# Token-id expert layer of a two-layer decoder: operands as exact sums of two 12-bit parts, products as three one-pass products of the parts, not native 32-bit ones

## The chip, the cores and the metric

The kernel runs on one core of one Trainium2 chip. The metric is device time in microseconds (us) for one execution. Times are medians of runs; the profile is of one execution.

## The reference, cut to what matters

The program is a decoder of two layers with six sublayers, each followed by a residual sum and a layer norm: a gated linear recurrence (stage A in the kernel), the token-id expert layer (B), a mixture of experts (C), window attention (D), a quantised product with the context (E), and latent attention with experts (F, G). The change is in stage B only:

```
expert_ids = jnp.minimum(tid // tokens_per_expert, E - 1)      # E = 4, one expert for each token
for e in range(E):
    g = jax.nn.silu(jnp.einsum('bsd,fd->bsf', hidden_states, Wg[e]))
    u = jnp.einsum('bsd,fd->bsf', hidden_states, Wu[e])
    y = jnp.einsum('bsf,df->bsd', g * u, Wd[e])
    out = jnp.where((expert_ids == e)[..., None], y, out)
...
x = _layernorm(x + _L0_xattn_ref(x, itok_BxS_13_99985, ctx_2048, ctx_2048, ctx_2048), axis=-1)
```

There are 2048 tokens of 512 features. All three weights of expert e are the same 512 x 512 matrix (ctx_2048[e]), so one product with it gives both g and u, and a second product with it gives y. The hidden value is silu(v) * v, which the kernel takes as (1 + tanh(v/2)) * v * v, with the factor 1/2 put into the residual sum.

## The kernel before, in words

Stage A has sorted the tokens by expert into 19 tiles of 128 rows (TILES_B = 19), each of one expert, has loaded the four transposed matrices into w (128 partitions x 4 experts x 4 chunks x 512, float32), and has left the tables row, who and tile_expert. An all-engine barrier ends it. Stage B is tokenid_expert_layer. No planner sets its order: each engine has its instructions in the order written, and semaphores tie the engines together.

- POOL (GpSimd) gathers tile n's rows of x1 into xg, a ring of four (AHEAD = 4, line 707). gather(n + 4) is issued after the sum of tile n is made (sum_ready) and, since POOL works in order, behind the small power for the inverse deviation of tile n (line 719). It scatters the finished rows into x2 (line 712).
- PE (TensorE) works in rounds. Round n holds, in this order: turn_x(n + 1), four transposes of 128x128 (line 765); turn_h(n - 1), four transposes (line 774); first_product(n), four calls of a 128x128 by 128x512 product (line 786); second_product(n - 1), four calls (line 796). The expert's number is read into a register, which addresses w.
- DVE (VectorE) in its loop for n: keep_xT(n + 1), the copy of the transposed rows out of PSUM (line 823); normalise(n - 2) (line 844); hidden(n) (line 827); moments(n - 1), which is the residual sum (line 832, it frees xg for the next gather), the statistics (835, 836) and the addition of epsilon (837).
- ACT (ScalarE): keep_hT(n - 1), the copy of the transposed hidden rows (line 749), then tanh and square of the first product of n (lines 741, 742).

PSUM has two buffers for each of the four uses (banks 0 to 7). Stage C begins after stage B's barrier.

Of the kernel before, what the change touches and what calls it, by code (L numbers as in the profile page):

```python
# [15 lines left out]
P = 128  # L16
# [3 lines left out]
KD = D // P  # L20
# [4 lines left out]
F32 = mybir.dt.float32  # L25
BF16 = mybir.dt.bfloat16
# [637 lines left out]
def tokenid_expert_layer(nc, d, x1, x2, route, ident):  # L664
# [5 lines left out]
    with stage_of(nc) as ctx:  # L670
# [6 lines left out]
        def sems(name):  # L677
# [3 lines left out]
        w, who, row, tile_expert = route  # L681
        power = sb("power", [P, 1])
        xg = [sb(f"xg{j}", [P, D]) for j in range(AHEAD)]
        res, y = ([sb(f"{n}{j}", [P, D]) for j in range(AHEAD)] for n in ("res", "y"))
        xgT, hT = ([sb(f"{n}{j}", [P, KD, P]) for j in (0, 1)] for n in ("xgT", "hT"))
# [5 lines left out]
        (x_turned, xT_ready, product1, th_ready, sq_ready, h_ready, h_turned, hT_ready, product2, sum_ready, var_ready, rstd_ready,  # L691
         y_ready) = (sem(n) for n in (
            "x_turned", "xT_ready", "product1", "th_ready", "sq_ready", "h_ready", "h_turned", "hT_ready", "product2",
            "sum_ready", "var_ready", "rstd_ready", "y_ready"))
        dve_step, power_ready = sem("dve_step"), sem("power_ready")
# [38 lines left out]
        @block.scalar  # L734
        def _(act):
            def squares(n):
                act.wait_ge(product1, n + 1)
                if n >= 2:

                    act.wait_ge(h_turned, n - 1)  # L740
                nc.scalar.activation(th[n % 2][:], ps[:, 2 + n % 2, :], ACT.Tanh, scale=0.5).then_inc(th_ready, 1)
                nc.scalar.activation(sq[n % 2][:], ps[:, 2 + n % 2, :], ACT.Square).then_inc(sq_ready, 1)

            def keep_hT(n):
                act.wait_ge(h_turned, n + 1)
                if n >= 2:

                    act.wait_ge(product2, n - 1)
                nc.scalar.copy(hT[n % 2][:], ps[:, 4 + n % 2, :].rearrange("p (k m) -> p k m", k=KD)).then_inc(hT_ready, 1)

            for n in range(TILES_B + 1):
                if n >= 1:
                    keep_hT(n - 1)
                if n < TILES_B:
                    squares(n)

        @block.tensor
        def _(pe):
            def turn_x(n):
                pe.wait_ge(gathered[n % AHEAD], 16 * (n // AHEAD + 1))  # L760
                if n >= 2:

                    pe.wait_ge(xT_ready, n - 1)
# [4 lines left out]
            def turn_h(n):  # L768
                pe.wait_ge(h_ready, n + 1)
                if n >= 2:  # L770

                    pe.wait_ge(hT_ready, n - 1)
# [6 lines left out]

            def first_product(n, e):  # L780
                pe.wait_ge(xT_ready, n + 1)
                if n >= 2:

                    pe.wait_ge(sq_ready, n - 1)
                for k in range(KD):
                    last = nc.tensor.matmul(ps[:, 2 + n % 2, :], xgT[n % 2][:, k, :], w[:, bass.ds(e, 1), k, :],
                                            start=(k == 0), stop=(k == KD - 1))
                last.then_inc(product1, 1)

            def second_product(n, e):  # L790
                pe.wait_ge(hT_ready, n + 1)
# [3 lines left out]
                for k in range(KD):  # L795
                    last = nc.tensor.matmul(ps[:, 6 + n % 2, :], hT[n % 2][:, k, :], w[:, bass.ds(e, 1), k, :],
                                            start=(k == 0), stop=(k == KD - 1))
                last.then_inc(product2, 1)

            e_now = expert(0)  # L800
            turn_x(0)
            for n in range(TILES_B + 1):
# [12 lines left out]
        def _(dve):  # L815
            steps = Steps(dve, dve_step)

            def keep_xT(n):
                dve.wait_ge(x_turned, n + 1)
# [3 lines left out]
                nc.vector.tensor_copy(xgT[n % 2][:], ps[:, n % 2, :].rearrange("p (k m) -> p k m", k=KD)).then_inc(xT_ready, 1)  # L823
# [23 lines left out]
            keep_xT(0)  # L847
            for n in range(TILES_B):
                if n + 1 < TILES_B:
                    keep_xT(n + 1)  # L850
# [5 lines left out]
            normalise(TILES_B - 2)  # L856
            moments(TILES_B - 1)
# [2711 lines left out]
```

## Time and profile before

| | |
|---|---|
| median of 3 runs | 2498.16 us (2497.85 to 2498.19) |
| profiled execution, first to last instruction (the only time that is kept of it) | 2498.3 us |
| busy share: PE, PE weight load, DVE, ACT, POOL | 90%, 41%, 55%, 26%, 28% |
| stage B, first gather to last scatter's issue | 391.8 to 552.3 us |
| lines 786 and 796, the two products: records of each | 152 (8 for each tile) |

How to read it: "PE" rows are matmuls, "PEld" rows the loads of the stationary operand, which overlap them. A matmul's listed duration includes the time through the array, so matmuls in a row overlap each other; what one costs in a row of them is the distance between starts. A float32 product of this form appears as two records. TensorE's clock has two levels, 1.2 and 2.4 GHz; the profile gives the granted share, 0.50 or 1.00, or a mean. In a timeline row the columns are start, duration, engine, line, operation, output <- inputs, count, and in brackets the idle time before it with what ended it. The program's span is the sum of its stages; between stages stands a barrier.

### The profile page before, as it was taken

How to read it: one execution, taken by the hardware profiler on the slowest of the kernel's cores; microseconds unless marked ns; L12 is line 12 of the kernel's file. 1: busy time of each engine (PE TensorE's matmuls, PEld its weight loads, DVE VectorE, ACT ScalarE, POOL GpSimd, SP SyncE). 2: the span in 40 equal slices, each digit the busy share in tenths (PEclk: the TensorE clock that was granted, in tenths of full speed). 3: DMA queues.
4: the chain of work that ended last, by engine and by line, in shares of the span. 5: the costliest groups of instructions: out<-in, count | busy, mean ns of one | idle time of the engine just before them, and what ended most of it. 6: DMA issues, size and time to landing. Idle time of an engine off the chain costs nothing. (4 is left out here: it accounts for less than half of the span.)

```text
span 2498.3 us, 29517 instructions
## 1 busy us (share of the span) xinstructions
PE 2247.5 (90%) x10083; PEld 1030.3 (41%) x10086; DVE 1381.1 (55%) x3181; ACT 657.9 (26%) x1163; POOL 695.2 (28%) x1018
## 2 busy tenths in 40 slices
PE   9999997979999999898999997478888888799993
PEld 4444443435444443344444443233333333344441
DVE  6999883436412223555766774955656564422224
ACT  2222321212012121233434333433322322002223
POOL 2210002324523321133433333011113131125553
PEclk9999998999999999998999998689999999999997
DMA  8333102126047776163443330310000000064444
GB/s 293 117 101 112 40 4 72 64 76 243 10 133 247 236 234 202 40 165 83 90 85 78 84 71 2 109 71 1 2 18 2 18 27 18 17 199 83 87 88 149
DMA packets 101697, 235.40 MB, mean 94 GB/s; under 512 B 18919, under 2 KB 42647, under 8 KB 94399
## 3 DMA queue, kind: packets, MB, share of 16 engines
q1 hardware_dynamic: 79006, 191.83, 24.4%
q0 software_dynamic: 22560, 41.87, 7.7%
q8 instruction: 77, 1.26, 0.2%
q14 instruction: 54, 0.43, 0.1%
HBM read 174.69 MB, written 63.53 MB: 95 GB/s over the span
## 5 line engine op out<-in xcount | busy, mean ns | idle before, releaser
L1876 DVE CUSTOM_DVE_ANT_0 D_ps<-D_ps,D_mask 128x256 f32<-128x256 f32 (+1 forms) x512 | 186.9, 420 | 70.7 <-PE D_ps L1773 69.7
L1625 POOL TENSOR_SCALAR_AFFINE_SELECT D_probs<-D_probs 128x256 f32<-128x256 f32 x256 | 106.1, 420 | 286.7 <-ACT D_probs L1683 286.4
L1683 ACT ACTIVATE D_probs<-D_ps 128x512 f32<-128x512 f32 (+1 forms) x256 | 125.3, 543 | 165.0 <-PE D_ps L1795 164.8
L2876 DVE TENSOR_REDUCE F_neg_max<-F_ps 128x4 f32<-128x2048 f32 (+1 forms) x64 | 93.9, 1488 | 107.7 <-PE F_ps L2774 101.6
L3318 PE MATMUL G_ps<-G_gate_up,G_xgT 128*128 x304 | 138.5, 599 | 0.3 <-DVE G_xgT L3409 0.3
L2626 ACT ACTIVATE F_probs<-F_ps 128x1536 f32<-128x1536 f32 (+1 forms) x48 | 76.4, 1591 | 187.2 <-PE F_ps L2790 187.2
L1186 PE MATMUL C_ps<-C_down_shared,C_hs 128*128 128x512 f32 x256 | 114.0, 593 | 3.4 <-DVE C_hs L1353 2.3
L1174 PE MATMUL C_ps<-C_xT,C_gate_shared 128*128 128x512 f32 x256 | 115.4, 593 | 0.6 <-ACT C_xT L1049 0.6
L1174 PE MATMUL C_ps<-C_xT,C_up_shared 128*128 128x512 f32 x256 | 115.1, 592 | 0.0
L1773 PE MATMUL D_ps<-D_k_stack,D_q_stack 96*128 96x256 bf16 (+1 forms) x512 | 93.4, 268 | 8.8 <-DVE D_maxima L1876 7.2
L1023 POOL DMA_INDIRECT expert_sums<-C_y,C_of_slot x32 | 50.2, 1570 | 173.4 <-ACT C_y L1090 108.9
L2507 POOL TENSOR_SCALAR_AFFINE_SELECT F_probs<-F_probs 128x512 f32<-128x512 f32 x64 | 41.0, 652 | 179.7 <-ACT F_probs L2626 179.7
L3417 DVE SCALAR_TENSOR_TENSOR G_tile_gu<-G_tile_th,G_ps 128x256 f32<-128x256 f32 x38 | 16.0, 421 | 129.9 <-ACT G_tile_th L3230 129.9
L374 PE MATMUL A_ps<-A_u,A_wa 128*128 128x512 f32 x200 | 86.5, 592 | 0.0
L374 PE MATMUL A_ps<-A_u,A_wi 128*128 128x512 f32 x200 | 86.5, 592 | 0.0
L1795 PE MATMUL D_ps<-D_q_stack,D_k_stack 99*128 99x256 bf16 (+1 forms) x512 | 75.3, 272 | 12.3 <-DMA D_q_stack<-D_m_lo 12.3
L1811 PE MATMUL D_ps<-D_probs,D_v 128*32 128x256 f32 (+1 forms) x1024 | 78.2, 378 | 6.5 <-POOL D_probs L1627 4.8
L1005 POOL DMA_INDIRECT slots<-C_entry,C_address x64 | 64.3, 1004 | 55.2 <-DVE C_address L1338 36.6
L1773 PEld LDWEIGHTS D_ps<-D_k_stack,D_q_stack 96*128 96x128 bf16 x512 | 44.6, 101 | 84.3 <-issue 51.2
L3318 PEld LDWEIGHTS G_ps<-G_gate_up,G_xgT 128*128 128x128 f32 x304 | 55.4, 192 | 56.1 <-issue 56.1
L1627 POOL TENSOR_SCALAR_AFFINE_SELECT D_probs<-D_probs 128x256 f32<-128x256 f32 x192 | 77.9, 406 | 0.0
L1795 PEld LDWEIGHTS D_ps<-D_q_stack,D_k_stack 99*128 99x128 bf16 x512 | 47.3, 101 | 67.9 <-issue 39.5
(496 smaller groups left out, 4531.1 us busy)
## 6 DMA issues: line engine op xcount, KB each, us to landing
C_ring<-moe_experts_dram SPq DMA_DIRECT2D x32, 1536.0 KB, 6.9
qk_parts<-D_parts SPq DMA_DIRECT2D x32, 384.0 KB, 2.5
B_w<-ctx_dram SPq DMA_DIRECT2D x8, 1024.0 KB, 6.0
expert_sums<-A_cq SPq DMA_DIRECT2D x1, 8192.0 KB, 29.4
C_ring<-expert_sums SPq DMA_DIRECT2D x5, 1536.0 KB, 10.4
D_q_stack<-qk_parts SPq DMA_DIRECT2D x16, 384.0 KB, 4.8
D_k_stack<-qk_parts SPq DMA_DIRECT2D x16, 384.0 KB, 7.7
B_w<-ctxT_dram SPq DMA_DIRECT2D x1, 4096.0 KB, 15.9
```

The lines of the kernel that those rows point to most:

```text
L374: last = nc.tensor.matmul(ps[:, tile % 8, :], w[:, k, m * P:(m + 1) * P], moving[:, k, :], start=(k == 0), stop=(k == chunks - 1))
L1174: last = nc.tensor.matmul(ps[:, bank + part, :], w_shared[part][:, k, f:f + P], xT[:, k, g * S:(g + 1) * S], start=(k == 0), stop=(k == KD ...
L1186: last = nc.tensor.matmul(ps[:, 2 + c % 2, :], hs[:, m, i * P:(i + 1) * P], down_shared[:, s * KF + m, :], start=(m == 0), stop=(m == KF - 1))
L1625: last = nc.gpsimd.affine_select(now[:, :, 0:P], now[:, :, 0:P], [[0, 2], [1, P]], ALU.is_ge, 0.0, base=0, channel_multiplier=-1)
L1627: last = nc.gpsimd.affine_select(now[:, :, P:2 * P], now[:, :, P:2 * P], [[0, 2], [-1, P]], ALU.is_ge, 0.0, base=0, channel_multiplier=1)
L1683: nc.scalar.activation(probs[at % 2][:, 2 * pair:2 * pair + 2, 0:w], ps[:, 4 + unit % 3, :].rearrange("p (h q) -> p h q", h=2)[:, :, 0:w], ...
L1773: last = nc.tensor.matmul(ps[:, 2 + u % 2, h * 256 + first:(h + 1) * 256], q_stack[0:STACK, head, t * P:(t + 1) * P], k_stack[0:STACK, hea ...
L1795: last = nc.tensor.matmul(bank[:, h * 256:h * 256 + w], k_stack[:, head, kb * P:(kb + 1) * P], q_stack[:, head, kb * P:kb * P + w], start= ...
L1811: last = nc.tensor.matmul(ps[h * (P // 4):(h + 1) * (P // 4), 7, kb * P:kb * P + w], v[b % 2][:, kb, c * HC + 4 * g + h, :], probs[at % 2] ...
L1876: last = nc.vector.tensor_tensor_reduce(now, now, mask[:, first:256], 1.0, -3e38, ALU.add, ALU.max, maxima[n % 2][:, head, t:t + 1])
L2876: last = nc.vector.tensor_reduce(neg_max[n % 2][:, :, t], ps[:, 0:GROUP, at:at + w], AX_X, ALU.max, negate=True)
L3318: last = nc.tensor.matmul(ps[:, 2 + a, :], xgT[a][:, k, :], gate_up[:, bass.ds(e, 1), k, :], start=(k == 0), stop=(k == KD - 1))
```

## The change

A product is then hi*hi + hi*lo + lo*hi, all in the float32r type, accumulated in one PSUM bank: 12 matmul calls in place of 4. The transposes stay float32.

- The weights are split once at the stage's head: four copies of 128x2048 on ACT, four subtractions on DVE. PE waits for all of them (w_lo_ready) after turn_x(0).
- For each tile ACT makes x_hi from PSUM (high_x) and h_hi in place of hT (high_h). DVE makes x_lo in place of the copy xgT (low_x), and h_lo (low_h), each after the high part.
- The last third of each product waits for the low part. In DVE's last steps low_h(18) stands behind normalise(17).

```
--- before.py
+++ after.py
@@ -23,6 +23,7 @@
 EPS = 1e-5
 
 F32 = mybir.dt.float32
+F32R = mybir.dt.float32r
 BF16 = mybir.dt.bfloat16
 I32 = mybir.dt.int32
 U32 = mybir.dt.uint32
@@ -679,20 +680,22 @@
 
         E, AHEAD = EXPERTS_B, 4
         w, who, row, tile_expert = route
+
+        w_hi, w_lo = (sb(n, [P, E, KD, D], F32R) for n in ("w_hi", "w_lo"))
         power = sb("power", [P, 1])
         xg = [sb(f"xg{j}", [P, D]) for j in range(AHEAD)]
         res, y = ([sb(f"{n}{j}", [P, D]) for j in range(AHEAD)] for n in ("res", "y"))
-        xgT, hT = ([sb(f"{n}{j}", [P, KD, P]) for j in (0, 1)] for n in ("xgT", "hT"))
+        x_hi, x_lo, h_hi, h_lo = ([sb(f"{n}{j}", [P, KD, P], F32R) for j in (0, 1)] for n in ("x_hi", "x_lo", "h_hi", "h_lo"))
         th, sq = ([sb(f"{n}{j}", [P, D]) for j in (0, 1)] for n in ("th", "sq"))
         stats, mv, rstd = sb("stats", [P, 6]), sb("mv", [P, TILES_B, 2]), sb("rstd", [P, TILES_B])
         ps = ctx.enter_context(nc.psum_tensor("B_ps", [P, 8, 512], F32))
 
         gathered, stored = sems("gathered"), sems("stored")
-        (x_turned, xT_ready, product1, th_ready, sq_ready, h_ready, h_turned, hT_ready, product2, sum_ready, var_ready, rstd_ready,
-         y_ready) = (sem(n) for n in (
-            "x_turned", "xT_ready", "product1", "th_ready", "sq_ready", "h_ready", "h_turned", "hT_ready", "product2",
-            "sum_ready", "var_ready", "rstd_ready", "y_ready"))
-        dve_step, power_ready = sem("dve_step"), sem("power_ready")
+        (x_turned, x_hi_ready, x_lo_ready, product1, th_ready, sq_ready, h_ready, h_turned, h_hi_ready, h_lo_ready, product2,
+         sum_ready, var_ready, rstd_ready, y_ready) = (sem(n) for n in (
+            "x_turned", "x_hi_ready", "x_lo_ready", "product1", "th_ready", "sq_ready", "h_ready", "h_turned", "h_hi_ready",
+            "h_lo_ready", "product2", "sum_ready", "var_ready", "rstd_ready", "y_ready"))
+        dve_step, power_ready, w_hi_ready, w_lo_ready = (sem(n) for n in ("dve_step", "power_ready", "w_hi_ready", "w_lo_ready"))
         block = ctx.enter_context(nc.Block(no_gpsimd_drain=True))
 
         @block.gpsimd
@@ -741,16 +744,28 @@
                 nc.scalar.activation(th[n % 2][:], ps[:, 2 + n % 2, :], ACT.Tanh, scale=0.5).then_inc(th_ready, 1)
                 nc.scalar.activation(sq[n % 2][:], ps[:, 2 + n % 2, :], ACT.Square).then_inc(sq_ready, 1)
 
-            def keep_hT(n):
+            def high_x(n):
+                act.wait_ge(x_turned, n + 1)
+                if n >= 2:
+
+                    act.wait_ge(product1, n - 1)
+                nc.scalar.copy(x_hi[n % 2][:], ps[:, n % 2, :].rearrange("p (k m) -> p k m", k=KD)).then_inc(x_hi_ready, 1)
+
+            def high_h(n):
                 act.wait_ge(h_turned, n + 1)
                 if n >= 2:
 
                     act.wait_ge(product2, n - 1)
-                nc.scalar.copy(hT[n % 2][:], ps[:, 4 + n % 2, :].rearrange("p (k m) -> p k m", k=KD)).then_inc(hT_ready, 1)
-
+                nc.scalar.copy(h_hi[n % 2][:], ps[:, 4 + n % 2, :].rearrange("p (k m) -> p k m", k=KD)).then_inc(h_hi_ready, 1)
+
+            for e in range(E):
+                nc.scalar.copy(w_hi[:, e].rearrange("p k n -> p (k n)"), w[:, e].rearrange("p k n -> p (k n)")).then_inc(w_hi_ready, 1)
+            high_x(0)
             for n in range(TILES_B + 1):
+                if n + 1 < TILES_B:
+                    high_x(n + 1)
                 if n >= 1:
-                    keep_hT(n - 1)
+                    high_h(n - 1)
                 if n < TILES_B:
                     squares(n)
 
@@ -760,7 +775,7 @@
                 pe.wait_ge(gathered[n % AHEAD], 16 * (n // AHEAD + 1))
                 if n >= 2:
 
-                    pe.wait_ge(xT_ready, n - 1)
+                    pe.wait_ge(x_lo_ready, n - 1)
                 for k in range(KD):
                     last = nc.tensor.transpose(ps[:, n % 2, k * P:(k + 1) * P], xg[n % AHEAD][:, k * P:(k + 1) * P], ident[:])
                 last.then_inc(x_turned, 1)
@@ -769,7 +784,7 @@
                 pe.wait_ge(h_ready, n + 1)
                 if n >= 2:
 
-                    pe.wait_ge(hT_ready, n - 1)
+                    pe.wait_ge(h_lo_ready, n - 1)
                 for k in range(KD):
                     last = nc.tensor.transpose(ps[:, 4 + n % 2, k * P:(k + 1) * P], sq[n % 2][:, k * P:(k + 1) * P], ident[:])
                 last.then_inc(h_turned, 1)
@@ -777,28 +792,34 @@
             def expert(n):
                 return pe.value_load(tile_expert[0:1, n:n + 1], min_val=0, max_val=E - 1)
 
+            def three_products(out, hi, lo, lo_ready, n, e):
+
+                for k in range(KD):
+                    nc.tensor.matmul(out, hi[:, k, :], w_hi[:, bass.ds(e, 1), k, :], start=(k == 0), stop=False)
+                for k in range(KD):
+                    nc.tensor.matmul(out, hi[:, k, :], w_lo[:, bass.ds(e, 1), k, :], start=False, stop=False)
+                pe.wait_ge(lo_ready, n + 1)
+                for k in range(KD):
+                    last = nc.tensor.matmul(out, lo[:, k, :], w_hi[:, bass.ds(e, 1), k, :], start=False, stop=(k == KD - 1))
+                return last
+
             def first_product(n, e):
-                pe.wait_ge(xT_ready, n + 1)
+                pe.wait_ge(x_hi_ready, n + 1)
                 if n >= 2:
 
                     pe.wait_ge(sq_ready, n - 1)
-                for k in range(KD):
-                    last = nc.tensor.matmul(ps[:, 2 + n % 2, :], xgT[n % 2][:, k, :], w[:, bass.ds(e, 1), k, :],
-                                            start=(k == 0), stop=(k == KD - 1))
-                last.then_inc(product1, 1)
+                three_products(ps[:, 2 + n % 2, :], x_hi[n % 2], x_lo[n % 2], x_lo_ready, n, e).then_inc(product1, 1)
 
             def second_product(n, e):
-                pe.wait_ge(hT_ready, n + 1)
+                pe.wait_ge(h_hi_ready, n + 1)
                 if n >= 2:
 
                     pe.wait_ge(sum_ready, n - 1)
-                for k in range(KD):
-                    last = nc.tensor.matmul(ps[:, 6 + n % 2, :], hT[n % 2][:, k, :], w[:, bass.ds(e, 1), k, :],
-                                            start=(k == 0), stop=(k == KD - 1))
-                last.then_inc(product2, 1)
+                three_products(ps[:, 6 + n % 2, :], h_hi[n % 2], h_lo[n % 2], h_lo_ready, n, e).then_inc(product2, 1)
 
             e_now = expert(0)
             turn_x(0)
+            pe.wait_ge(w_lo_ready, E)
             for n in range(TILES_B + 1):
                 if n + 1 < TILES_B:
                     e_next = expert(n + 1)
@@ -815,12 +836,21 @@
         def _(dve):
             steps = Steps(dve, dve_step)
 
-            def keep_xT(n):
-                dve.wait_ge(x_turned, n + 1)
+            def low_x(n):
+                dve.wait_ge(x_hi_ready, n + 1)
                 if n >= 2:
 
                     dve.wait_ge(product1, n - 1)
-                nc.vector.tensor_copy(xgT[n % 2][:], ps[:, n % 2, :].rearrange("p (k m) -> p k m", k=KD)).then_inc(xT_ready, 1)
+                nc.vector.tensor_tensor(x_lo[n % 2][:], ps[:, n % 2, :].rearrange("p (k m) -> p k m", k=KD), x_hi[n % 2][:].bitcast(F32),
+                                        ALU.subtract).then_inc(x_lo_ready, 1)
+
+            def low_h(n):
+                dve.wait_ge(h_hi_ready, n + 1)
+                if n >= 2:
+
+                    dve.wait_ge(product2, n - 1)
+                nc.vector.tensor_tensor(h_lo[n % 2][:], ps[:, 4 + n % 2, :].rearrange("p (k m) -> p k m", k=KD), h_hi[n % 2][:].bitcast(F32),
+                                        ALU.subtract).then_inc(h_lo_ready, 1)
 
             def hidden(n):
                 dve.wait_ge(sq_ready, n + 1)
@@ -844,16 +874,23 @@
                 nc.vector.tensor_scalar(y[n % AHEAD][:], res[n % AHEAD][:], mv[:, n, 0:1], rstd[:, n:n + 1],
                                         ALU.subtract, ALU.mult).then_inc(y_ready, 1)
 
-            keep_xT(0)
+            for e in range(E):
+                dve.wait_ge(w_hi_ready, e + 1)
+                nc.vector.tensor_tensor(w_lo[:, e].rearrange("p k n -> p (k n)"), w[:, e].rearrange("p k n -> p (k n)"),
+                                        w_hi[:, e].rearrange("p k n -> p (k n)").bitcast(F32), ALU.subtract).then_inc(w_lo_ready, 1)
+            low_x(0)
             for n in range(TILES_B):
                 if n + 1 < TILES_B:
-                    keep_xT(n + 1)
+                    low_x(n + 1)
+                if n >= 1:
+                    low_h(n - 1)
                 if n >= 2:
                     normalise(n - 2)
                 hidden(n)
                 if n >= 1:
                     moments(n - 1)
             normalise(TILES_B - 2)
+            low_h(TILES_B - 1)
             moments(TILES_B - 1)
             normalise(TILES_B - 1)
```

## Rows read from the trace of the kernel before

**Rows 1.** Stretches: length, busy PE, PEld, DVE, ACT, POOL, clock, DMA, GB/s.

```profile
474.58:482.32 7.74, 7.74 (x26) 3.87 (x25) 3.58 (x8) 1.67 (x3) 2.84 (x3) 1.00 0.20 68
396.87:402.34 5.47, 5.47 (x13) 2.81 (x14) 0.99 (x2) 0.00 (x0) 0.00 (x0) 0.71 0.21 79
```

**Rows 2.** Timeline of one round in the middle of stage B.

```profile
473.70 0.60 PE L765 MATMUL B_ps<-ident,B_xg 128*128 128x128 f32 x4
473.90 0.69 DVE L832 SCALAR_TENSOR_TENSOR B_res<-B_ps,B_xg 128x512 f32<-128x512 f32 x1 [1.63 <-PE B_ps L796]
474.14 0.60 PE L774 MATMUL B_ps<-ident,B_sq 128*128 128x128 f32 x4
474.58 3.60 PE L786 MATMUL B_ps<-B_w,B_xgT 128*128 x8
...
476.56 1.28 POOL L707 DMA_INDIRECT B_xg<-x,B_row  x1 [0.19 <-issue]
478.01 3.60 PE L796 MATMUL B_ps<-B_w,B_hT 128*128 x8
...
481.45 0.60 PE L765 MATMUL B_ps<-ident,B_xg 128*128 128x128 f32 x4
```

**Rows 3.** Line 707's gathers issued between 470 and 500 us.

```profile
DMA to landing us min/median/max: 3.6/3.7/3.8
```

**Rows 4.** Timeline of one-pass bf16 products at 256 columns (stage D).

```profile
1102.70 0.61 PE L1795 MATMUL D_ps<-D_q_stack,D_k_stack 99*128 99x256 bf16 x4 [1.00 <-DMA D_q_stack<-D_m_lo]
1103.14 0.28 PE L1773 MATMUL D_ps<-D_k_stack,D_q_stack 96*128 96x128 bf16 x2
```

**Rows 5.** Timeline of bf16 transposes at full clock (stage E).

```profile
1592.64 1.07 PE L2087 MATMUL E_turned<-E_ident,E_xq 128*128 128x128 bf16 x16 [2.70 <-DVE E_xq L2126]
```

**Rows 6.** Weight loads by tile in stage B: count, ns min/median/max, starts, forms.

```profile
L786 PEld LDWEIGHTS B_ps<-B_w,B_xgT x152: 190/190/333, 397.6 to 538.7; 128*128 128x128 f32 x152
L774 PEld LDWEIGHTS B_ps<-ident,B_sq x76: 139/140/143, 404.4 to 543.2; 128*128 128x128 f32 x76
```

**Rows 7.** Groups by line and shape: busy us, mean ns, idle before.

```profile
L538 DVE TENSOR_TENSOR B_w<-B_w 128x2048 f32<-128x2048 f32 x4 | 9.2, 2292 | 0.1
L2025 ACT ACTIVATE E_work<-rows,E_scale 128x2048 f32<-128x2048 f32 x4 | 8.0, 2016 | 21.2 <-DVE E_scale L2110 21.2
L1857 DVE TENSOR_TENSOR D_rest<-D_ps,D_parts 128x512 f32<-128x512 f32 x32 | 22.1, 690 | 29.2 <-ACT D_parts L1654 29.2
L749 ACT COPY B_hT<-B_ps 128x512 f32<-128x512 f32 x19 | 11.1, 585 | 58.6 <-PE B_ps L774 58.6
```

**Rows 8.** Timeline of the end of stage A and the head of B.

```profile
387.47 0.32 SPq L271 DMA_DIRECT2D x<-A_y  x1
391.79 1.19 POOL L707 DMA_INDIRECT B_xg<-x,B_row  x1 [4.93 <-issue]
...
396.87 1.11 PE L765 MATMUL B_ps<-ident,B_xg 128*128 128x128 f32 x4 [0.43 <-DMA B_xg<-x,B_row]
397.77 4.73 PE L786 MATMUL B_ps<-B_w,B_xgT 128*128 x8
...
402.34 0.60 PE L765 MATMUL B_ps<-ident,B_xg 128*128 128x128 f32 x4
...
404.40 0.66 PE L774 MATMUL B_ps<-ident,B_sq 128*128 128x128 f32 x4 [1.47 <-DVE B_sq L827]
...
411.76 0.60 PE L765 MATMUL B_ps<-ident,B_xg 128*128 128x128 f32 x4
```

**Rows 9.** Line 271's four stores at the end of stage A.

```profile
DMA to landing us min/median/max: 2.0/2.2/2.5
```

**Rows 10.** Timeline of the end of stage B.

```profile
544.23 3.70 PE L796 MATMUL B_ps<-B_w,B_hT 128*128 x8 [0.68 <-ACT B_hT L749]
...
545.66 0.55 DVE L844 TENSOR_SCALAR B_y<-B_res,B_mv,B_rstd 128x512 f32<-128x512 f32 x1 [0.69 <-POOL B_rstd L719]
...
547.96 0.69 DVE L832 SCALAR_TENSOR_TENSOR B_res<-B_ps,B_xg 128x512 f32<-128x512 f32 x1 [1.75 <-PE B_ps L796]
```

## The prediction

> **What bounds the kernel now.** I read the page of the profile first, then, for the stretch of stage B alone, the busy time by stretches, the groups by line, PE's waits and the timeline. The page calls PE busy for 90% of the span, but that is a mean over seven stages and the change touches one, so the first thing to see is a window of one round of stage B: 7.74 us long, PE busy for all 7.74 at a granted clock of 1.00 (2.4 GHz), DVE 3.58, ACT 1.67, POOL 2.84 [rows 1]. PE sets the period there. The timeline of a round shows how it is made up: four transposes take 0.44 us (473.70 to 474.14), the next four 0.44, the first product 3.43 (474.58 to 478.01), the second 3.44, and the next round starts at 481.45, a period of 7.75 [rows 2]. Each product is eight records, so a record costs 3.43 / 8 = 0.429 us for 512 columns, and a call two of them, 0.858.
>
> The second thing to see is what stands just behind PE. The residual sum frees the gather ring; it starts 0.20 us after the round's end (473.90), and the gather of the tile four further on is issued at 476.56, 2.86 us after the end [rows 2]. It lands 3.7 us later (3.6 to 3.8) [rows 3], at 6.56. Its transposes are due after one more round, at 7.75. So the gather has 1.2 us to spare today, and a shorter period uses that up.
>
> **The change, part by part.**
>
> *A pass.* In place of 8 records of 0.429 us a product has 12 of an unknown price p. The trace has no float32r product. Lower bound: four bf16 passes of 256 columns start 0.44 us apart from the next group (1102.70 to 1103.14), 0.11 each, hence 0.22 for 512 columns [rows 4]; and a native call divided by four is 0.858 / 4 = 0.2145. Upper bound: the only single-record 32-bit operations, the transposes, take 0.11 us for 128 columns [rows 2], where 16 bf16 transposes take 1.07 us with the last one's run-out, under 0.07 each [rows 5]. If 32-bit words of any kind move at that pace, p is 0.429. 
>
> The Trainium skill ("FP8 and Floating Point Precision", section TensorE Precision Notes) says that a true float32 product is four passes and that a reduced one reads four bytes and cuts them to 22 bits. By that rule three products of parts cost 3/4 of the native one; the native records, 0.858 for a call, agree with a count of four, and no run yet shows the reduced one.
>
> *Weight loads.* Each pass needs its own load. Loads take 190 ns in the native product and 139 ns in the transposes [rows 6], both under 214, and they overlap the matmul before. So they stay hidden; with no such cover the 139 would be added to every pass (below nothing is gained: the loads are hidden already).
>
> *Register work and waits on PE.* The second waits (for the low part) fall where the low part is ready: low_x(n) is made a round ahead, low_h(n - 1) as worked out next. In the trace no idle time stands between the transposes and the register-addressed product [rows 2], so I put the addresses at nothing; if 12 calls outran PE's sequencer, it would show as a larger p.
>
> *DVE and ACT in a round.* low_x replaces a copy at the same price, a subtraction of 128x512 out of PSUM, 690 ns; low_h adds one more, so DVE has 3.58 + 0.69 = 4.3 us. ACT has 1.67 + 0.59 = 2.3 us for one more copy of 585 ns [rows 1, 7]. Both lie under any period above. In order of time from the end of a round: moments until 2.0, low_x 2.7, low_h 3.5, normalise 4.1. PE wants h_lo at 0.88 + 2.57 + 1.72 = 5.2. It costs nothing, with 1.7 us of cover. The gather's path (sum, statistics, POOL) is ahead of all that was added, so it stays at 2.86 + 3.7.
>
> *The period.* PE alone: 0.88 + 24 x 0.2145 = 6.03 us. The gather lands 6.56 after the end of round n + 1, and turn_x(n + 4) opens round n + 3, which then takes 6.03 itself. Two rounds so cost 6.56 + 6.03, a period of 6.30. What was hidden becomes a wait of about 0.5 us before every second round's transposes (or half of it before each). Seventeen rounds, 2 to 18: 17 x (7.75 - 6.30) = 24.6 us gained; by PE alone 17 x 1.72 = 29.2.
>
> *The head.* PE waits for four low parts of the weights. DVE's subtraction of 128x2048 takes 2.29 us; the nearest row for the copy is an ACT activation from SBUF of the same size, 2.02 [rows 7]. DVE waits for the first copy only, so the split lasts 2.02 + 4 x 2.29 + 0.1 = 11.3 us. It starts with the stage, after the last store of stage A lands: 387.47 + 2.2 = 389.7 at the earliest, 391.79 (POOL's first gather) at the latest [rows 8, 9]; I take 390.3. PE enters round 0 at 401.6, not at 396.87: 4.8 us late (4.2 to 6.3). Round 0 took 5.47 us at a mean granted clock of 0.71 [rows 1] for 0.44 + 3.43 = 3.87 us of full-clock work, so 3.2 us of it ran at 1.2 GHz. PE is idle ahead of it again, so I keep these 3.2: 0.44 + 2.57 + 1.6 = 4.6 us, 0.9 less (if the clock doesn't rise at all, 6.0). Round 1 took 9.42 (402.34 to 411.76), with 2.06 from its start until the hidden rows are ready [rows 8]. Now 2.06 + 0.44 + 5.15 = 7.65, 1.8 less. The head together: +4.8 - 0.9 - 1.8 = +2.1.
>
> *The tail.* The last second product ran from 544.23, and its sum began at 547.96 [rows 10]. low_h(18) stands behind normalise(17), which ends at 545.66 + 0.55 = 546.21 on the old scale; h_lo comes at 546.9, four passes take 0.86, the sum starts at 548.0. With its first eight passes done long before, this costs 0.1 us.
>
> Sum: +2.1 - 24.6 + 0.1 = -22.4. The profiled execution's span is 2498.3 us, the median 2498.16, so 2475.8 by the median; I say 2476. The later stages start after a barrier and only move forward.
>
> **Rivals.**
> 1. *No wait for the gather* (it lands sooner, or the loop closes in another way): +2.1 - 29.2 + 0.1 = -27, 2471. For it: landings of 3.3 us would cut the period to 6.1. Against: none between 470 and 500 us was under 3.6 [rows 3].
> 2. *32-bit words move at half pace*, the one on the other side. p = 0.429, period 0.88 + 24 x 0.429 = 11.2: 17 x 3.4 = +58, head +4.8 + 1.7 + 3.4, tail +1.6, together +70, 2568. For it: the transposes [rows 2, 5]. The sum has p some 450 times (12 + 24 + 408 and the tail), so from -27 at 0.2145 it turns at 0.2145 + 27 / 450 = 0.274 us.
> 3. *Weight loads come into the open:* p = 0.2145 + 0.139 = 0.354, period 9.4, +36 together, 2534. Against: a load starts one matmul ahead today and is shorter than a pass [rows 6].
> 4. *The change doesn't do what it says:* a float32r call is run as a native one, 0.858. The period is 21.5, over 230 us slower, above 2730.
> 5. *Passes closer than their columns.* From the native rows, eight records of 0.429 leave no room for it [rows 2]; a pass of 0.131 would make PE's round 4.0, the gather's loop (6.56 + 4.0) / 2 = 5.3, and the whole 43 us faster, 2455. The Trainium skill ("TensorE: Matmul & The Clock Gate", section Back-to-back issue gap) gives such a 131 ns for streams of load and matmul at 512 columns; the trace disagrees, 0.2145 for a quarter of a call.
>
> **How the numbers follow.** Forecast 0.56, rival 1 0.22, rival 2 0.12, rival 3 (with smaller exposures or a slow sequencer) 0.06, rivals 4 and 5 0.01 each, and 0.02 for a p near 0.274, where gain and loss cancel. The forecast's own bounds: stage start and cold round +1.5 + 1.4 and -0.6, landings of 4.2 us in busier queues +4.3 (period 6.55). That gives 2475 to 2483; with rival 1 below it and some play on either side, 2468 to 2486 holds just under 8 in 10. A difference under 0.2% (5 us) is about what a measurement of this kernel can't tell from none. Faster 0.80, within it 0.02, slower 0.18.
>
> **What the changed profile would show.** In the middle of stage B: 12 records for each product, starts 0.21 apart, weight loads under 0.2 us; the granted clock at 1.00; a period of 6.2 to 6.4 with PE idle for the gather in line with the transposes of x, 0.2 to 0.6 us. At the head: four ACT copies of about 2.0, four DVE subtractions of 2.29, the first product at about 402.5, not 397.8. At the end: low_h(18) right behind normalise(17). The prediction is wrong if the records are 0.4 apart, if idle time stands ahead of each load, if PE waits for h_lo, or if the clock drops in mid-stage.

## The result, and the profile after

| | before | changed | ratio to before, 95% interval |
|---|---|---|---|
| first comparison | 2498.19 us (2497.85 to 2504.62) | 2487.24 us (2481.16 to 2489.70) | 0.9938 (0.9921 to 0.9955) |
| second | 2496.25 | 2485.66 | 0.9945 (0.9923 to 0.9967) |
| third | 2497.14 | 2479.85 | 0.9930 (0.9911 to 0.9948) |

The change makes the kernel 0.6% faster: 0.0062 x 2498.16 is 15.5 us, between 11.2 and 19.7. The forecast was 22.4 less, 2476 in a range of 2468 to 2486; by the ratio it is 2482.7, while the median of the changed kernel's own runs, 2487.24, lies 1.2 above that range. A second run of the unchanged kernel before came out at 1.0014 (1.0000 to 1.0028).

The profiled execution of the changed kernel has a span of 2479.4 us, against 2498.3. Its stage B lasts from 392.84 (the first gather) to 535.85 (the start of the last scatter), 143.0 us; the kernel before has 391.79 to 551.31, 159.5 us (the 552.3 in the table ahead of the prediction is the end of that last scatter's instruction). So 16.5 us came out of stage B, in that trace; in two more of the changed kernel B took 142.7 and 143.5, in a second one of before 160.4. The rest of the span's difference lies in stages that the change does not touch: stage C took 494.5 and 498.5 us in two traces of before, 491.7, 498.0 and 491.8 in three of the changed kernel; D goes from 513.6 to 517.5 in these five. B is read from traces to about 1 us, a whole execution is not.

The page of the changed kernel, busy time by engine: DVE rises from 55% to 57%, ACT from 26% to 27%.

```profile
PE 2218.7 (89%) x10235; PEld 1054.4 (43%) x10238; DVE 1401.2 (57%) x3204; ACT 675.1 (27%) x1186; POOL 695.5 (28%) x1018
```

One round in the middle of stage B, timeline of the changed kernel (line 780 is turn_x, 789 turn_h, 798/800/803 the three groups of passes, 852 low_h, 862 the sum, 710 the gather). It answers to [rows 2].

```profile
462.38 0.60 PE L780 MATMUL B_ps<-ident,B_xg 128*128 128x128 f32 x4
462.58 0.69 DVE L862 SCALAR_TENSOR_TENSOR B_res<-B_ps,B_xg 128x512 f32<-128x512 f32 x1 [0.99 <-PE B_ps L803]
...
463.17 1.18 PE L798 MATMUL B_ps<-B_w_hi,B_x_hi 128*128 x4
464.19 1.10 PE L800 MATMUL B_ps<-B_w_lo,B_x_hi 128*128 x4
464.94 0.68 DVE L852 TENSOR_TENSOR B_h_lo<-B_ps,B_h_hi 128x512 fp32r<-128x512 f32 x1
465.12 1.10 PE L803 MATMUL B_ps<-B_w_hi,B_x_lo 128*128 x4
465.25 1.01 POOL L710 DMA_INDIRECT B_xg<-x,B_row  x1 [0.19 <-issue]
...
466.05 1.10 PE L798 MATMUL B_ps<-B_w_hi,B_h_hi 128*128 x4
...
467.92 1.10 PE L803 MATMUL B_ps<-B_w_hi,B_h_lo 128*128 x4
```

No row of PE has a bracket: PE does not wait in this round. Four passes start 0.93 us after the four before them (464.19 to 465.12), which is 0.234 a pass and not 0.2145. The first product takes 2.88 us (463.17 to 466.05), and the round 6.47. h_lo is there at 465.6, 2.3 us before it is used.

Windows of the changed kernel over round 0 and over rounds 2 to 18 (columns as in [rows 1]), and PE's waits in the stage (us in total, times, longest):

```profile
403.22:408.94 5.72, 5.72 (x17) 4.64 (x18) 0.69 (x1) 0.59 (x1) 0.00 (x0) 0.53 0.01 5
417.09:527.37 110.28, 109.89 (x541) 89.93 (x540) 68.95 (x135) 36.26 (x67) 41.97 (x49) 1.00 0.23 74
```

```profile
PE B_ps L780 <- DMA B_xg<-x,B_row: 11.4, 2, 11.0
PE B_ps L780 <- DVE B_w_lo L879: 5.6, 1, 5.6
PE B_ps L789 <- DVE B_sq L857: 1.5, 1, 1.5
PE B_ps L798 <- ACT B_h_hi L759: 0.7, 1, 0.7
PE B_ps L803 <- DVE B_h_lo L852: 0.5, 1, 0.5
```

In 110.28 us PE is busy for 109.89: PE's own work sets the period. The first row of the waits is the very first gather (11.0) and one wait of 0.4 near the end; the last two rows are the last tile. In line with that the gathers issued between 470 and 500 us land sooner than in [rows 3], and only those issued after 500 us land late:

```profile
DMA to landing us min/median/max: 3.2/3.4/3.6
...
DMA to landing us min/median/max: 3.6/3.9/4.2
```

The head of the stage, timeline of the changed kernel, for [rows 8]:

```profile
391.69 7.30 ACT L762 CAST B_w_hi<-B_w 128x2048 fp32r<-128x2048 f32 x4 [39.87 <-PEq L92]
392.84 1.19 POOL L710 DMA_INDIRECT B_xg<-x,B_row  x1 [4.92 <-issue]
393.62 8.90 DVE L879 TENSOR_TENSOR B_w_lo<-B_w,B_w_hi 128x2048 fp32r<-128x2048 f32 x4 [5.12 <-ACT B_w_hi L762]
394.33 2.40 POOL L710 DMA_INDIRECT B_xg<-x,B_row  x1 [0.30 <-issue]
...
403.22 1.11 PE L780 MATMUL B_ps<-ident,B_xg 128*128 128x128 f32 x4 [5.64 <-DVE B_w_lo L879]
...
405.84 1.91 PE L800 MATMUL B_ps<-B_w_lo,B_x_hi 128*128 x4
...
408.94 0.60 PE L780 MATMUL B_ps<-ident,B_xg 128*128 128x128 f32 x4
411.00 0.66 PE L789 MATMUL B_ps<-ident,B_sq 128*128 128x128 f32 x4 [1.47 <-DVE B_sq L857]
...
417.09 0.60 PE L780 MATMUL B_ps<-ident,B_xg 128*128 128x128 f32 x4
```

The split lasts from 391.69 to 402.5, and PE enters round 0 at 403.22, with the wait on the low parts of the weights named in the bracket.

### The profile page after: what moved, and what is told of

It is laid out like the page before. It is cut to its first block and busy times, and to the rows that moved or that the text cites. A ratio compares the mean times of both kernels' runs of the same rounds, so it can differ in the third digit from the quotient of the medians.

```text
span 2479.4 us, 29975 instructions
## 1 busy us (share of the span) xinstructions
PE 2218.7 (89%) x10235; PEld 1054.4 (43%) x10238; DVE 1401.2 (57%) x3204; ACT 675.1 (27%) x1186; POOL 695.5 (28%) x1018
```

## The experiments

Stage B's length (first gather to start of last scatter) and the distance of the rounds come from each kernel's trace; the expectation of same_again counts to the end of the last scatter's instruction, which is 1.0 us more. Theory: the period is PE's work at 0.234 us a pass, and the rest of what is missing against the forecast is the head. Rivals: the gather loop still sets the period; register addressing or weight loads make up the extra 0.02 us of a pass; the head costs another amount.

| kernel | ratio to before | stage B, us | a round in mid-stage, us |
|---|---|---|---|
| before, two traces | 1.0014 (second) | 159.5, 160.4 | 7.74 |
| changed, three traces | 0.9938, 0.9945, 0.9930 | 143.0, 142.7, 143.5 | 6.46 to 6.51 |
| half_columns | one execution, 2465.89 us | 122.4 | 6.3 and 4.7 in turn |
| eight_passes | 0.9856 (0.9833 to 0.9879) | 122.2 | 6.2 and 4.7 in turn |
| ring6 | 0.9962 (0.9947 to 0.9977) | 141.0 | 6.46 |
| fixed_expert | one execution, 2479.75 us | 143.1 | 6.46 |
| bf16_parts | 0.9922 (0.9896 to 0.9949) | 136.3 | 6.2 |
| split_only | 1.0031 (1.0019 to 1.0044) | 165.8 | 7.74 |
| native_head, two | 0.9917 (0.9901 to 0.9933), 0.9934 (0.9913 to 0.9955) | 139.0, 140.1 | 6.46 |

**The changed kernel and the kernel before again** (same_again, changed_third, before_again), to learn what varies between executions.

> The changed kernel once more, unaltered, because its five times lie between 2481.2 and 2489.7 us and its profile is of the fastest. If the gain sits in stage B alone and the rest of the spread is the clock's timing in other stages, stage B lasts from the first gather to the last scatter's issue 144.0 us as in the first profile (392.8 to 536.9), within 1 us, while stage C or later differs by up to some 6 us at unequal mean granted clocks. If the spread is made in stage B (gathers that land late in some executions), B itself differs by several us, with PE waiting for gathers in rounds. Median 2483 to 2489 either way.

> The changed kernel a third time, beside native_head on the same chip. B at 143 us (142.5 to 143.5); ratio to the kernel before 0.993 to 0.995, which is B's gain of 16.6 us (0.9934) with the scatter of the other stages on top. If the change also costs something outside B, the ratio stays above 0.995 over all three sets of times.

> The kernel before, unaltered, for a second profile. So far stage B took 159.5 us (first gather to last scatter's issue) in the only profile before and 143.1 and 142.7 in two of the changed kernel, while stage C and D varied by 7 us and more between profiles of all variants. If that variation is none of the change's, this profile has B within 0.5 us of 159.5 and C or D off by 1 to 7 us from the first profile (494.5 and 515.5).

Stage B repeats within 0.9 us for each kernel, and the three ratios of the changed kernel have a mean of 0.9938. Stages C and D don't repeat so well.

**half_columns**: the eight passes with a low part take 256 columns; half of the correction is left out.

```
-  nc.tensor.matmul(out, hi[:, k, :], w_lo[:, bass.ds(e, 1), k, :], ...)
+  nc.tensor.matmul(out[:, 0:256], hi[:, k, :], w_lo[:, bass.ds(e, 1), k, 0:256], ...)
-  last = nc.tensor.matmul(out, lo[:, k, :], w_hi[:, bass.ds(e, 1), k, :], ...)
+  last = nc.tensor.matmul(out[:, 0:256], lo[:, k, :], w_hi[:, bass.ds(e, 1), k, 0:256], ...)
```

> The eight passes of each product that use a low part run over 256 of the 512 columns only (half of the correction of the result is left out); the four hi*hi passes keep 512. Every pass keeps its weight load. Theory A, the pass of 0.234 us is set by its weight load (PEld 187 to 190 ns): the 256-column passes also start 0.234 us apart and the period stays at 6.47 us. Theory B, the pass is its columns and a fixed 0.02 us: the narrow ones start 0.12 to 0.13 us apart, PE's round is 0.79 + 8 x 0.234 + 16 x 0.127 = 4.7 us, and the period is then set by the gather, (6.4 + 4.7) / 2 = 5.5 us. Under A the time is that of the changed kernel, under B about 16 us less.

Timeline of the second product of a round of half_columns, and of the transposes of the next round:

```profile
460.12 1.10 PE L798 MATMUL B_ps<-B_w_hi,B_h_hi 128*128 x4
461.06 0.64 PE L800 MATMUL B_ps<-B_w_lo,B_h_hi 128*128 x4
461.54 0.63 PE L803 MATMUL B_ps<-B_w_hi,B_h_lo 128*128 x4
463.15 0.66 PE L780 MATMUL B_ps<-ident,B_xg 128*128 128x128 f32 x4 [0.98 <-DMA B_xg<-x,B_row]
```

Four passes of 512 columns are 0.94 apart (460.12 to 461.06), four of 256 are 0.48 apart. A pass follows its columns: 0.12 us for 256, 0.235 for 512. If a load set the pace, the shorter pass would not have come out at half. So rival 3 of the prediction is out. And now that PE's round is short, the gather wait that was forecast for the changed kernel appears. The stage is 20.7 us shorter than the changed kernel's, where 16 were expected: rounds 0 and 1, which the expectation left out, are 3.2 us shorter as well (4.32 and 6.36 in place of 5.72 and 8.15).

**eight_passes**: the two mixed groups are replaced by one, lo*lo; a third of the work is left out.

```
-  for k in range(KD):
-      nc.tensor.matmul(out, hi[:, k, :], w_lo[:, bass.ds(e, 1), k, :], ...)
   pe.wait_ge(lo_ready, n + 1)
   for k in range(KD):
-      last = nc.tensor.matmul(out, lo[:, k, :], w_hi[:, bass.ds(e, 1), k, :], ...)
+      last = nc.tensor.matmul(out, lo[:, k, :], w_lo[:, bass.ds(e, 1), k, :], ...)
```

> Each product has eight passes, hi*hi and lo*lo; the two mixed terms are left out. PE's own round is then 0.79 + 16 x 0.234 = 4.53 us. If the gather closes a loop over two rounds, as the prediction has it (issue 2.86 us after a round's end, 3.4 us to land), the period is (6.4 + 4.5) / 2 = 5.5 us with PE idle for the gathers, 17 x 0.95 = 16 us below the changed kernel. If the gather is no bound, 4.53 and 33 us below. If the gather closes a loop over one round, the period stays at 6.4.

Timeline of eight_passes, the starts of turn_x in three rounds:

```profile
452.80 0.66 PE L780 MATMUL B_ps<-ident,B_xg 128*128 128x128 f32 x4 [1.60 <-DMA B_xg<-x,B_row]
...
457.45 0.60 PE L780 MATMUL B_ps<-ident,B_xg 128*128 128x128 f32 x4
...
463.73 0.66 PE L780 MATMUL B_ps<-ident,B_xg 128*128 128x128 f32 x4 [1.51 <-DMA B_xg<-x,B_row]
```

Every second round waits for a gather, for 1.5 us, the rounds between run at PE's own 4.65, and two rounds take 10.93. This is the loop of the prediction's period: a gather lands 6.28 us after the end of a round, the round that follows its transposes takes 4.65, and half of the sum is 5.47. So the loop is real; in the changed kernel PE's round, 6.47, is longer than the 6.28, and no wait is left. (That the stage is 20.8 us shorter and not 16 has the same reason as in half_columns: rounds 0 and 1.)

**ring6**: a ring of six gather buffers.

```
-        E, AHEAD = EXPERTS_B, 4
+        E, AHEAD = EXPERTS_B, 6
```

> The gather ring (and the rings of the sum and of the finished rows) has six buffers instead of four, so a gather is issued two rounds earlier against its use. The changed kernel's period is 6.467 us; its passes and transposes add up to 0.79 + 24 x 0.234 = 6.41. If the gather holds the rounds up, the period falls to 6.41 (1 us in all) and the PEld waits for the gather go; if the passes alone set it, nothing changes. Total within 1 us of the changed kernel in both, so the trace decides, not the time.

The waits of PE in ring6 show that the one small wait for a gather is gone and nothing else:

```profile
PE B_ps L780 <- DMA B_xg<-x,B_row: 11.1, 1, 11.1
```

The rounds stay at 6.46 and stage B is 2 us shorter. Of these, 1.1 are in round 0 (4.58 in place of 5.72 us, at a granted clock of 0.69 in place of 0.53, which the ring has no part in) and 0.7 in the last two rounds, which no longer wait. A whole execution doesn't show it (0.9962, its stage D took 521.4 us).

**fixed_expert**: the weights are addressed with the constant 3; the choice of the expert is left out.

```
-  w_hi[:, bass.ds(e, 1), k, :]
+  w_hi[:, 3, k, :]          # w_lo likewise
```

> All tiles use expert 3 at a fixed address, so no pass is addressed through a register (the choice of the expert is left out). The passes of the changed kernel start 0.234 us apart where four make up a native call at 0.2145 each. If the register addressing (a register operation ahead of a matmul) is the 0.02 us, the passes here start 0.214 apart, PE's round is 0.79 + 24 x 0.2145 = 5.94 us and the period about (6.3 + 5.9) / 2 = 6.1. If it isn't, 0.234 and 6.47 stay.

Timeline of fixed_expert, two groups of four passes:

```profile
462.68 1.09 PE L800 MATMUL B_ps<-B_w_lo,B_x_hi 128*128 128x512 f32 x4
463.61 1.09 PE L803 MATMUL B_ps<-B_w_hi,B_x_lo 128*128 128x512 f32 x4
```

Still 0.93 for four. Register addressing costs these passes nothing.

**bf16_parts**: the parts are bfloat16, so they hold 8 bits each.

```
-  w_hi, w_lo = (sb(n, [P, E, KD, D], F32R) for n in ("w_hi", "w_lo"))
+  w_hi, w_lo = (sb(n, [P, E, KD, D], BF16) for n in ("w_hi", "w_lo"))   # x_hi, x_lo, h_hi, h_lo likewise
```

> The high and low parts are bf16 in place of float32r (8 bits of mantissa for each part, so the sum keeps 16 and not 24 bits); all else is the same, 24 passes in a round with their register addresses. If the 0.02 us over 0.2145 belong to streaming 32-bit words, the passes start 0.215 us apart, the loads are about 0.10 us, the period is near 6.1 (PE 5.95, gather loop (6.3 + 5.95) / 2) and the time 5 to 7 us below the changed kernel's. If they come from addressing or from the many short calls, 0.234 and 6.47 stay.

Timeline of bf16_parts, two groups of four passes and the transposes of two rounds:

```profile
459.34 0.64 PE L780 MATMUL B_ps<-ident,B_xg 128*128 128x128 f32 x4
...
461.12 1.03 PE L800 MATMUL B_ps<-B_w_lo,B_x_hi 128*128 x4
461.98 1.03 PE L803 MATMUL B_ps<-B_w_hi,B_x_lo 128*128 x4
...
465.60 0.66 PE L780 MATMUL B_ps<-ident,B_xg 128*128 128x128 f32 x4
```

Here four passes take 0.86, so 0.2155 each: the pace that was forecast for float32r. The same columns, order and engines with two-byte words run at 0.2155, with float32r words at 0.234. Stage B is 6.8 us shorter than in the changed kernel's first trace. With the faster pass PE's own round is 6.10, and the gathers' 2.87 + 3.3 = 6.2 lies just above it: rounds of 6.10 stand beside rounds of 6.15 to 6.44 (this one takes 6.26), with a mean of 6.2. So the forecast wait is there, but only as 0.3 us or less.

**split_only**: the kernel before with the change's head alone. It makes the parts of the weights and waits for them, and the products stay native.

```
+            for e in range(E):
+                nc.scalar.copy(w_hi[:, e]..., w[:, e]...).then_inc(w_hi_ready, 1)
...
             turn_x(0)
+            pe.wait_ge(w_lo_ready, E)
...
+            for e in range(E):
+                dve.wait_ge(w_hi_ready, e + 1)
+                nc.vector.tensor_tensor(w_lo[:, e]..., w[:, e]..., w_hi[:, e]..., ALU.subtract).then_inc(w_lo_ready, 1)
             keep_xT(0)
```

> The kernel before with only the split of the weights and PE's wait for it put in; the products stay native and don't use the parts. The prediction put the head's delay at 4.8 us (PE enters round 0 at 401.6 and not at 396.9). In the changed kernel's trace it is 403.2 - 1.1 (stage A ended 1.1 us later there) - 396.9 = 5.3 us. So stage B should be 5.3 us longer than before, plus some 0.5 to 1 us if the longer idle time ahead of round 0 makes more of it run at 1.2 GHz; the total about 5.5 to 6 us above the kernel before. If the split runs in the shade of something else, 0.

Stage B is 6.3 us longer than in the first trace of before and 5.5 longer than in the second: round 0 starts 5.3 us later after the first gather and itself takes 6.49 us, where it took 5.47 and 6.24. The whole kernel is slower by 0.31% (0.19 to 0.44), which is 4.7 to 11.0 us. The delay of round 0 is paid in full.

**native_head** (run twice): six gather buffers, and the first two tiles take the native product straight from w while ACT and DVE split the weights beside them. PE waits for the parts ahead of tile 2 only; low_h(18) goes ahead of normalise(17).

```
+  E, AHEAD, NATIVE = EXPERTS_B, 6, 2
...
   def first_product(n, e):
+      if n < NATIVE:
+          pe.wait_ge(x_lo_ready, n + 1)
+          native_product(ps[:, 2 + n % 2, :], x32[n], n, e).then_inc(product1, 1)
+          return
+      if n == NATIVE:
+          pe.wait_ge(w_lo_ready, E)
...
   turn_x(0)
-  pe.wait_ge(w_lo_ready, E)
```

> A version meant to beat both: tiles 0 and 1 take the native products from w while ACT and DVE split the weights, tiles 2 to 18 the three products of parts; the gather ring has six buffers; low_h(18) stands ahead of normalise(17). If the head costs what the traces say, round 2 starts as early as in the kernel before (20.0 us after the first gather, not 24.2), which is 4.3 us; 0.5 us from the last low part and 0.6 from the last two gathers, together 5.4 us below the changed kernel in stage B: 138 us from the first gather to the last scatter's issue, against 143. If the clock or DVE's queue eats it, 1 to 3 us.

> native_head again, for a comparison with the changed kernel on one chip. Its B was 139.0 us against 143.1 and 142.7, so 4 us below the changed kernel (ratio lower by 0.0016); if the difference of the first medians (2478.3 against 2485.7 and 2487.2) was mostly the other stages' scatter, it shrinks to that.

Timeline of native_head's head:

```profile
394.29 2.40 POOL L711 DMA_INDIRECT B_xg<-x,B_row  x1 [0.30 <-issue]
397.00 0.95 POOL L711 DMA_INDIRECT B_xg<-x,B_row  x1 [0.30 <-issue]
398.25 2.97 POOL L711 DMA_INDIRECT B_xg<-x,B_row  x1 [0.30 <-issue]
399.12 1.12 PE L783 MATMUL B_ps<-ident,B_xg 128*128 128x128 f32 x4 [1.65 <-DMA B_xg<-x,B_row]
400.03 4.68 PE L800 MATMUL B_ps<-B_w,B_x 128*128 x8
...
404.55 0.60 PE L783 MATMUL B_ps<-ident,B_xg 128*128 128x128 f32 x4
...
413.98 0.60 PE L783 MATMUL B_ps<-ident,B_xg 128*128 128x128 f32 x4
```

Round 0 starts at 399.12 and not at 403.22, the wait on B_w_lo is gone, and round 2 starts at 413.98 and not at 417.09. Stage B is 139.0 and 140.1 us, 3 to 4 us shorter than in the changed kernel. The expectation was 5.4 us: round 2 starts 21.2 us after the first gather and not 20.0, since the second gather (394.29) takes 2.40 us to issue and the transposes wait for it at 399.12; and round 2 takes 7.09 us, because the second product of tile 1, which falls into it, is still native. In the whole time this is not resolved: 0.9917 and 0.9934 against 0.9930 to 0.9945.

## Why the prediction came out as it did

The sign of the whole and its largest terms were right, the gain comes from PE's shorter rounds as forecast, and the size was too large; the wait for the gather, which was part of the forecast, did not come. Against the first gather's start the terms measure as follows.

| term | forecast, us | measured, us |
|---|---|---|
| start of round 0 | +4.8 | +5.30 (10.38 in place of 5.08) |
| round 0 | -0.9 | +0.25 (5.72 in place of 5.47) |
| round 1 | -1.8 | -1.27 (8.15 in place of 9.42) |
| rounds 2 to 18 | -24.6 | -20.9 (110.28 in place of 131.19) |
| tail | +0.1 | +0.1 (8.48 in place of 8.36) |
| sum | -22.4 | -16.5 |

**The term that was mis-sized** is the pass, by the choice "I take 0.2145". It measures 0.234, and outside round 0 it enters 444 times (24 in round 1, 17 x 24, 12 in the tail): 444 x 0.0195 is 8.7 us of PE's work. In round 0, at 1.2 GHz, the price was right, as the last section shows. fixed_expert and half_columns take the rivals for it away (register addresses, weight loads), and bf16_parts, at 0.2155 with nothing else changed, puts it on the float32r words (its loads are shorter too, 98 ns, but loads were ruled out by half_columns). It is also far from the other bound, 0.429: the parts don't move at the half pace of rival 2, and the change would have turned at 0.274.

The result lies inside the range, but the range was not made for this: its width came from the head and the landings, and a pass between 0.2145 and 0.274 had 0.02 of the chances. The miss stayed small because a forecast wait went away with it, as follows, and that is luck.

**The period.** PE's own round is 6.47: 0.79 of transposes, 2.88 and 2.80 of products (the first group of four behind the transposes takes 1.02, the others 0.93). A wait comes only where a gather lands later after a round's end than the next round lasts. The forecast had 6.56 against 6.03; measured are 2.87 (462.38 to 465.25) + 3.4 = 6.27 against 6.47, so the wait of 0.5 us in every second round didn't come. Only the last two rounds, whose gathers take up to 4.2 us to land, are longer, 6.54 and 7.08 us, with the 0.4 of wait shown above. Rival 1 (no wait for the gather) was right about the wait and wrong about the time that it would give, since its 29.2 us too hang on 0.2145. With 0.234 in place of 0.2145 the prediction's own working gives a PE round of 6.50, a period of (6.56 + 6.50) / 2 = 6.53 and 17 x (7.75 - 6.53) = 20.7 us for rounds 2 to 18; measured are 20.9. So the pass alone is enough to explain this row. One error hid part of the other: 17 x 24 x 0.0195 = 8.0 us were lost on the passes, and most of the 17 x 0.27 = 4.6 us of forecast wait came back. In bf16_parts and eight_passes PE's round, 6.10 and 4.65, is below the 6.2 to 6.3 of the gather, and there the wait appears, with up to 0.3 and with 1.5 to 1.6 us.

The gather's own term was a little high as well: a landing of 3.4, not 3.7. Its instruction on POOL took 1.02 us in place of 1.28 [rows 2]. In the kernel before, normalise begins on DVE at 476.41 and the gather at 476.56; in the changed kernel the gather begins first, at 465.25, and normalise at 465.54. The pairing holds in the other traces: 1.27 and 1.28 us with normalise first in split_only, 1.01 and 1.02 with the gather first in ring6, fixed_expert and bf16_parts. That this overlap is the cause was not tried.

**The head.** The split began 1.15 us ahead of the first gather and not 1.5. ACT's copies were cheaper than 2.02 (7.30 for four), and DVE's four subtractions took 8.90 in all, near the 9.2 forecast; then 0.7 us pass until PE's first transpose, which the forecast didn't have. The profile puts all of the idle time on B_w_lo; by the code PE also reads the number of the next expert there, but what that costs was not tried. For round 0 I had assumed that 3.2 us of it run at 1.2 GHz, as in [rows 1]. It ran at a granted clock of 0.53, so nearly all of it at 1.2 GHz, where it had been 0.71. The bound given there, 6.0 if the clock doesn't rise, was the nearer one: changed_third, at a granted clock of 0.50 through the whole round, took 6.03. This round is also the least steady of the stage: 5.72, 5.47 and 6.03 us in three traces of the changed kernel, 4.58 in ring6, 5.47 and 6.24 in two of before. Round 1 is off by the passes alone: 2.06 until the hidden rows, as forecast, and then 6.09 in place of 5.59.

**What was hidden stayed hidden.** Weight loads, by tile in stage B of the changed kernel, are as long as in [rows 6] and lie under passes of 234 ns:

```profile
L800 PEld LDWEIGHTS B_ps<-B_w_lo,B_x_hi x76: 187/188/331, 405.4 to 523.2; 128*128 128x128 f32 x76
```

DVE works 68.95 us of the 110.28, 4.06 a round against 4.3 forecast, and h_lo has 2.3 us of cover. Only in the last tile does PE wait for it. This is the tail in the timeline of the changed kernel, for [rows 10]:

```profile
528.64 1.20 PE L798 MATMUL B_ps<-B_w_hi,B_h_hi 128*128 x4 [0.68 <-ACT B_h_hi L759]
...
530.54 0.68 DVE L852 TENSOR_TENSOR B_h_lo<-B_ps,B_h_hi 128x512 fp32r<-128x512 f32 x1
...
531.28 1.19 PE L803 MATMUL B_ps<-B_w_hi,B_h_lo 128*128 x4 [0.52 <-DVE B_h_lo L852]
...
532.51 0.69 DVE L862 SCALAR_TENSOR_TENSOR B_res<-B_ps,B_xg 128x512 f32<-128x512 f32 x1 [1.28 <-PE B_ps L803]
```

The eight passes before it are fed, so 3.73 became 3.87: 0.1 us, as forecast.

By the count of passes in the Trainium skill ("FP8 and Floating Point Precision", section TensorE Precision Notes), three passes in place of four make 3/4. The trace agrees with the four (0.858 is four times 0.2145), but the pass itself is 9% dearer, so a round's products went from 6.86 to 5.68 us, 0.83 of it.

**What stays open.** Why a float32r pass takes 0.234 us where a bf16 one takes 0.2155, at equal columns and 2.4 GHz; the last section narrows it down but doesn't name the cause. And whether native_head beats the changed kernel: by its stage, yes; by whole executions it can't be said. How many bits a float32r word keeps, and so how exact the sum of the two parts is, no run here measures; the times don't depend on it.

## What to carry to other kernels

A gain worked out as a count of passes is worth no more than the price of one pass in the data type that will run, so measure that by a stream of the same shape before anything else: 9% on a pass is 8.7 us of PE's work here, where 16.5 were gained, and bf16_parts, with the cheaper pass, has a stage shorter by 6.8. When PE is shortened, work out the next loop in line and what it needs (here a gather must land within the next round: 6.27 us against 6.47); a small error in one decides whether the other shows at all. Work done once at a stage's head is paid in full when it stands ahead of the first product; tiles that don't need it can run in front of it.

## What the runs showed that was not expected

- float32r passes of 512 columns are 0.234 us apart at the full clock, bf16 ones 0.2155, a quarter of a native call 0.2145. At 1.2 GHz the difference is gone. The timeline of round 0 in changed_third, at a granted clock of 0.50 throughout, and in bf16_parts before its clock rises:

```profile
406.06 1.91 PE L800 MATMUL B_ps<-B_w_lo,B_x_hi 128*128 x4
407.77 1.89 PE L803 MATMUL B_ps<-B_w_hi,B_x_lo 128*128 x4
409.48 0.62 PE L780 MATMUL B_ps<-ident,B_xg 128*128 128x128 f32 x4
```

```profile
405.16 1.49 PE L798 MATMUL B_ps<-B_w_hi,B_x_hi 128*128 x3 [0.22 <-issue]
406.44 1.16 PE L800 MATMUL B_ps<-B_w_lo,B_x_hi 128*128 x4
```

Four float32r passes take 1.71 us (406.06 to 407.77, and again to 409.48), three bf16 ones 1.28 (405.16 to 406.44): 0.427 each for both, and the records of the native calls in round 0 of before_again are 0.853 apart, 0.427 a pass too. So the extra 0.02 is no fixed number of TensorE's cycles: half the clock would double it, and there it is nothing. It goes with the columns (0.12 for 256 in half_columns). The figures fit a limit that doesn't follow TensorE's clock, some 0.46 ns for a float32r column (0.234 / 512), which the 0.83 ns of the slower clock (0.427 / 512) hides. What it is was not tried. (The group at the head of a product, behind the transposes, takes longer than the others, 1.86 at 1.2 GHz from 403.98 to 405.84 and 1.02 at 2.4, and is no measure of a pass.)

- A gather's instruction on POOL takes 0.94 to 0.95 us at the head of the kernel before (behind the first one, 1.19) and 1.89 to 2.40 (2.97 in native_head) while DVE subtracts two 128x2048 tensors of SBUF. So gathers at the head land later than the count of instructions says; in the changed kernel this was covered by the wait for the parts, but in native_head it is what PE waits for at 399.12. In native_head the gather at 397.00, with ACT's copies but no subtraction beside it, takes 0.95 again. The Trainium skill ("GPSIMD Engine Reference", section Specifications) says that GpSimd shares its SBUF interfaces with VectorE and contends with its instructions that have two SBUF inputs. The rows agree: all the long ones lie beside such subtractions, and the short ones don't.
- Stages that the change doesn't touch differ by 4 to 6 us between executions of one program (C 494.5 and 498.5 in two traces of before, 491.7 and 498.0 in two of the changed kernel); D goes from 511.9 to 521.4 over all kernels of the study. For an effect of a few us the stage's own length in the trace is the better measure.
